# Batch 0 of a fused adapter and mixture-of-experts kernel: where its sums, its results and its small operands are kept, and when they are moved

## The reference, cut to what matters

```python
def reference(x, ids, lang, A0, B0, W, Wr, A, B):      # x: (8, 512, 2048) float32
    Bx = einsum('bni,bri->bnr', x, B0[ids])            # adapter of the batch element, rank 16
    x = x + einsum('bnr,bor->bno', Bx, A0[ids])        # first layer
    base = einsum('btd,od->bto', x, W)                 # W: (2048, 2048)
    logits = einsum('btd,ed->bte', x, Wr) + 5.0 * one_hot(lang, 8)[:, None, :]
    gates = softmax of the top 2 of 8 logits, scattered back to 8
    h = einsum('btd,erd->bter', x, A)                  # 8 experts of rank 16
    lora = einsum('bter,bte,eor->bto', h, gates, B)
    return x + base + 2.0 * lora                       # second layer
```

## Time and profile before

| | us |
|---|---|
| median of 3 runs | 1602.15 |
| lowest and highest | 1599.51, 1602.99 |
| the profiled execution's own time | 1606.35 |
| its span, first to last instruction | 1604.6 |
| PE busy (share of the span) | 1556.7 (97%) |
| DVE busy | 1221.7 (76%) |
| ACT busy | 713.9 (44%) |
| POOL busy | 126.2 (8%) |

### The profile page before, as it was taken

The page is one execution under the profiler, slowest core; times in us unless marked ns, Lnnn a source line. Parts: engine busy times, 40 slices in busy tenths (PEclk is TensorE's granted clock), DMA queues, the critical chain, the costliest instruction groups (busy, mean ns, idle before and its releaser), DMA issues.

```text
span 1604.6 us, 20300 instructions
## 1 busy us (share of the span) xinstructions
PE 1556.7 (97%) x7446; PEld 1308.1 (82%) x7446; DVE 1221.7 (76%) x1625; ACT 713.9 (44%) x908; POOL 126.2 (8%) x176
## 2 busy tenths in 40 slices
PE   8687999999999999999999999999999999999998
PEld 8565877888888888888888888888888888888887
DVE  5785675897678876987769976888769877797665
ACT  5432222254444544454444544455444544445443
POOL 1254454300000000000000000000000000000000
PEclk9898999999999999999999999999999999999999
DMA  9979998877677776677777776778866777576664
GB/s 235 254 212 233 220 267 211 231 223 220 199 238 218 227 221 204 223 217 225 207 221 229 218 217 199 229 218 237 217 211 221 212 229 203 190 235 201 206 221 159
DMA packets 332534, 351.37 MB, mean 219 GB/s; under 512 B 229834, under 2 KB 265978, under 8 KB 331642
## 3 DMA queue, kind: packets, MB, share of 16 engines
q1 hardware_dynamic: 323026, 318.61, 69.5%
q0 software_dynamic: 9136, 30.94, 6.1%
q10 hardware_dynamic: 272, 0.52, 0.1%
HBM read 280.75 MB, written 68.82 MB: 218 GB/s over the span
## 4 chain that ended last, share of the span: by engine, by line
PE 88%; DVE 5%; DMA 4%; ACT 1%; issue 1%; SPq 1%; POOL 0%; DVEq 0%; ACTq 0%; POOLq 0%
PE pb L808 26%; PE pb L809 26%; PE pb L810 26%; PE pb L372 4%; PE pb L374 3%; PE pb L526 2%; DMA xst<-in_x_dram 1%; DVE raw L674 1%; DMA t_scr<-ost 1%; DVE wl L804 1%; DMA b0n<-in_L_cond_B_dram 1%; ACT wh L800 1%; DVE pool_a L533 1%; SPq L659 0%; DMA an<-in_L_cond_A_dram 0%
## 5 line engine op out<-in xcount | busy, mean ns | idle before, releaser
L800 ACT CAST wh<-raw 128x1024 fp32r<-128x1024 f32 (+1 forms) x456 | 477.0, 1046 | 753.2 <-PE pb L810 738.0
L804 DVE TENSOR_TENSOR wl<-raw,wh 128x1024 fp32r<-128x1024 f32 (+1 forms) x456 | 559.6, 1227 | 286.6 <-ACT wh L800 285.2
L808 PE MATMUL pb<-wh,sh 128*128 128x512 f32 x1568 | 612.9, 391 | 0.5 <-DVE ost L846 0.5
L809 PE MATMUL pb<-wl,sh 128*128 128x512 f32 x1568 | 611.6, 390 | 0.0
L810 PE MATMUL pb<-wh,sl 128*128 128x512 f32 x1568 | 611.2, 390 | 0.0
L810 PEld LDWEIGHTS pb<-wh,sl 128*128 128x128 f32 x1568 | 294.3, 188 | 62.9
L808 PEld LDWEIGHTS pb<-wh,sh 128*128 128x128 f32 x1568 | 294.5, 188 | 56.3 <-DVE wl L804 0.9
L809 PEld LDWEIGHTS pb<-wl,sh 128*128 128x128 f32 x1568 | 294.6, 188 | 55.1
L372 PE MATMUL pb<-awb,xah 128*128 128x304 f32 x512 | 138.5, 304 | 0.0
L374 PE MATMUL pb<-awb,xal 128*128 128x256 f32 x512 | 134.4, 280 | 0.0
L808 PE MATMUL pb<-wh,xh 128*128 128x512 f32 x256 | 105.6, 413 | 16.3 <-DVE ost L846 14.4
(11 more groups left out here) (149 smaller groups left out, 1286.1 us busy)
## 6 DMA issues: line engine op xcount, KB each, us to landing
raw<-t_scr SPq DMA_DIRECT2D x392, 512.0 KB, 3.8
xst<-in_x_dram SPq DMA_DIRECT2D x448, 64.0 KB, 3.6
out_dram<-ost SPq DMA_DIRECT2D x72, 256.0 KB, 3.4
raw<-in_L_cond_W_dram SPq DMA_DIRECT2D x124, 128.0 KB, 4.7
raw<-bt_scr SPq DMA_DIRECT2D x28, 512.0 KB, 3.5
out_dram<-u SPq DMA_DIRECT2D x56, 256.0 KB, 2.8
t_scr<-tst POOLq DMA_DIRECT2D x17, 512.0 KB, 5.5
t_scr<-raw POOLq DMA_DIRECT2D x32, 256.0 KB, 4.6
```

The lines of the kernel that those rows point to most:

```text
L800: e.copy(pair_split(wh, g), pair_source(g)).then_inc(c_wh, 1)
L804: e.tensor_tensor(out=pair_split(wl, g), in0=pair_source(g), in1=pair_split(wh, g).bitcast(f32), op=ALU.subtract).then_inc(c_wl, 1)
L808: e.matmul(o, h, wh[:, g % RING, k, :], start=start, stop=False)
L809: e.matmul(o, h, wl[:, g % RING, k, :], start=False, stop=False)
```

## The change

All of it is in batch 0 and the part before it.

1. **Six banks.** The results of chunk c go to the banks `(0, 1, 2, 3, 6, 7)[(4 * c + t) % 6]`. PE needs nothing evacuated for t = 0 and 1 of the next chunk; for t = 2 and 3 it waits for the evacuation of t = 0 and 1 of the chunk before. The transposes and deltas of batch 1 that used bank 6 use bank 5 or wait for its evacuation.
2. **Evacuation in two parts.** t = 0 and 1 are evacuated at the end of the chunk's last slot as before, t = 2 and 3 two slots later, both into `ost[:, 0:2]`; the second part waits for the stores of the first.
3. **W's sums** alternate strictly between `tst` and `ost[:, 2:4]`. POOL makes its two sums from the second pair on, not from the fourth.
4. **Gated rows** of chunk 0 are read from `bt` itself, those of chunks 1 and 2 from `btx`, a place of their own (it lies over `bxt`), so that they no longer take a turn of a raw place of W. The load of pair 10 waits for the transpose of pair 7, where before it waited for the split of the gated rows.
5. **ACT** copies the first and third step of the experts' B before it rounds the next pair of W.
6. **DVE before slot 0**: the transpose of pair 0 is moved ahead, `aux_sum` ahead of the last `a0_lo`, and the four sums of pair 0 to just behind the transpose of pair 1. ACT's rounding of pair 0 and `aux_low` are moved ahead too.
7. **The difference** of the experts' B is made by POOL in slot 6, no longer by DVE in slot 3.
8. **SP** loads the x of batch 1 a slot earlier, and its first two blocks in halves over slots 4 to 7.

The diff, cut to its core:

```diff
@@ bx_transpose, bx_keep, hg_hi, delta
+        def bx_bank(n):
+            return 5 if n == 1 else 6
@@ hg_hi, n == 0
-                e.wait_ge(d_btd, 16)
+                e.wait_ge(d_gs, 32)
+                e.wait_ge(d_ag, 48)
@@
+        def raw_turn(g):
+            return w_number(g) - (g > 2)
+
         def raw_place(g):
-            return (g + 1) % 2 if 3 <= g < 8 else g % 2
+            return raw_turn(g) % 2
@@ first_load
-            elif g == 9:
-                e.wait_ge(c_wc, 2 * w_number(6) + 2)
-            elif g >= 3:
-                before = {3: 0, 4: 1, 8: 7}.get(g, g - 2)
-                if before % 9 == 8:
-                    e.wait_ge(c_wl, before + 1)
-                else:
-                    e.wait_ge(c_wc, 2 * w_number(before) + 2)
...
+            elif raw_turn(g) >= 2:
+                before = raw_turn(g) - 2
+                e.wait_ge(c_wc, 2 * (before + (before >= 2)) + 2)
@@
         def sum_place(g):
-            return (0, 0, 0, 1, 0, 1, 0, 1)[g] if g < 8 else (1, 0, 0, 1, 0, 1, 0, 1)[g % 9]
+            return w_number(g) % 2
@@ w_sum
-            return ost[:, 0:2, :].rearrange("p t (s n) -> p (t s) n", s=2) if sum_place(g) else tst[:, :, :]
+            return ost[:, 2:4, :].rearrange("p t (s n) -> p (t s) n", s=2) if sum_place(g) else tst[:, :, :]
@@ w_sums
-            if w < 3:
+            if w == 0:
@@ pair_source
-            return raw[:, g % 2, 0, :] if i % 9 == 8 else w_kept(g).rearrange("p a n -> p (a n)")
+            if i % 9 != 8:
+                return w_kept(g).rearrange("p a n -> p (a n)")
+            return (bt[:, 0:CW], btx[:, :], btx[:, :], raw[:, raw_place(g), 0, :])[i // 9]
@@
+        def first_bank(c, t):
+            return (0, 1, 2, 3, 6, 7)[(4 * c + t) % 6]
+
+        def wait_first(e, c, t):
+            e.wait_ge((c_evd, c_eva)[t % 2], 2 * c + 1 + t // 2)
@@ first_products
-                if c and k == 0 and h == 0:
-                    e.wait_ge((c_evd, c_eva)[t % 2], 2 * c - 1 + t // 2)
+                if k == 0 and h == 0 and c and t >= 2:
+                    wait_first(e, c - 1, t - 2)
+                elif k == 0 and h == 0 and c >= 2:
+                    wait_first(e, c - 2, t + 2)
@@ first_evacuate
-            if c:
-                e.wait_ge(d_ost[t // 2], 32 * c)
-            if t < 2:
-                e.wait_ge(d_ts[1], sums_in(1, min(9 * c + 10, SLOTS0)))
+            if c == 3 and t >= 2:
+                e.wait_ge(d_ts[1], sums_in(1, SLOTS0))
+            elif c or t >= 2:
+                e.wait_ge(d_ost[0], 32 * (2 * c + t // 2))
@@
+        EVACUATED = {8: (0, 0), 10: (0, 2), 17: (1, 0), 19: (1, 2), 26: (2, 0), 28: (2, 2)}
@@ act_main
-                pair_hi(e, i + 2)
                 if i in (1, 2):
                     bt_copy(e, 2 * i - 2)
+                pair_hi(e, i + 2)
```

More of the change, by code:

```diff
@@ L116, in adapted_moe_lora_kernel @@
         st48 = sb("st48", [P, TT, P], f32)
+        s4 = ExitStack()
+        btx = sb("btx", [P, CW], f32, s4)
+        s4.close()
         bxt = sb("bxt", [P, T], f32r)
@@ L407, in bx_transpose @@
             for t in range(TT):
-                last = e.transpose(pb[:, 6, t * P:(t + 1) * P], st48[:, t, :], ident[:, :])
+                last = e.transpose(pb[:, bx_bank(n), t * P:(t + 1) * P], st48[:, t, :], ident[:, :])
             last.then_inc(c_gp, 1)
@@ L414, in bx_keep @@
                 e.wait_ge(c_dl, 16 * n)
-            e.copy(bxt[:, :], pb[:, 6, :]).then_inc(c_ga, 1)
+            if n == 1:
+                e.wait_ge(c_wl, 27)
+            e.copy(bxt[:, :], pb[:, bx_bank(n), :]).then_inc(c_ga, 1)
         def aux_adapted(e, n):
@@ L611, in w_number @@
             return g // 9 * 8 + g % 9
+        def raw_turn(g):
+            return w_number(g) - (g > 2)
         def raw_place(g):
-            return (g + 1) % 2 if 3 <= g < 8 else g % 2
+            return raw_turn(g) % 2
         def raw_in(g):
-            return sum(32 if n % 9 == 8 else 64 for n in range(g + 1) if n != 2 and raw_place(n) == raw_place(g))
+            return sum(32 if n == SLOTS0 - 1 else 64 for n in range(g + 1)
+                       if n != 2 and (n % 9 != 8 or n == SLOTS0 - 1) and raw_place(n) == raw_place(g))
         def raw_before(s):
@@ L702, in wait_sum_place @@
                 e.wait_ge(d_ts[n], sums_in(n, g))
-            if g == 3:
+            if g == 1:
                 e.wait_ge(c_bnj, E)
-            if n and g % 9 == 3 and g > 9:
-                e.wait_ge(d_ost[0], 32 * (g // 9))
         def w_blocks(g):
@@ L713, in w_sums @@
             b11, b12, b21, b22 = w_blocks(g)
-            done = 4 * w if w < 3 else 2 * w + 6
+            done = 2 * w + 2 if w else 0
             e.wait_ge(c_wc, 2 * w + 2)
@@ L1156, in bt_half @@
             return bt[:, :].rearrange("p (c w n) -> p w c n", c=4, w=2)[:, w, :, :]
+        bt_diff = pool_a[:, 3, 0:4, :]
         def bt_difference(e):
             e.wait_ge(c_btc, 4)
-            e.wait_ge(d_gs, 32)
-            e.wait_ge(d_ag, 48)
-            e.tensor_tensor(out=late[:, :].rearrange("p (c n) -> p c n", c=4), in0=bt_half(0), in1=bt_half(1),
-                            op=ALU.subtract).then_inc(c_btc, 1)
+            e.wait_ge(c_l0, 16)
+            e.tensor_tensor(out=bt_diff, in0=bt_half(0), in1=bt_half(1), op=ALU.subtract).then_inc(c_btd, 1)
         def bt_store(e):
@@ L1170, in bt_difference_store @@
         def bt_difference_store(e):
-            e.wait_ge(c_btc, 5)
-            e.dma_start(bt_scr[:, 2, :], late[:, :]).then_inc(d_btd, 16)
+            e.wait_ge(c_btd, 1)
+            e.dma_start(bt_scr[:, 2, :].rearrange("p (c n) -> p c n", c=4), bt_diff).then_inc(d_btd, 16)
         def bias_columns(e):
@@ L1325, in pool_main @@
                 sums = i + 2 < SLOTS0 and (i + 2) % 9 != 8
-                if sums and i:
+                if sums:
                     w_sum_3(e, i + 2)
@@ L1329, in pool_main @@
                     w_store(e, i + 3)
-                if sums and i:
+                if sums:
                     w_sum_2(e, i + 2)
-                if sums:
                     w_sums_store(e, i + 2)
@@ L1622, in sp_main @@
                     pair_load(e, i + 6)
-                if i % 9 == 8:
+                if i in EVACUATED:
+                    for t in range(2):
+                        first_store(e, EVACUATED[i][0], EVACUATED[i][1] + t)
+                if i == 35:
                     for t in range(TT):
-                        first_store(e, i // 9, t)
+                        first_store(e, 3, t)
             for b in range(1, NB):
@@ L1643, in sp_main @@
             for c in range(2):
-                e.wait_ge(d_ost[c], 128 + 64 * (NB - 1))
+                e.wait_ge(d_ost[c], OST0[c] + 64 * (NB - 1))
                 e.wait_ge(d_u2[c], 32 * (NB - 1))
```

97 lines of the change are left out of this document (60 added, 37 removed).

## The result

The changed kernel takes 1584.08 us (median of 4 runs, 1581.45 to 1584.87) against 1602.57 us for the kernel before in the same session (4 runs, 1599.51 to 1605.93). The ratio is 0.9881, 95% interval 0.9858 to 0.9904: faster by 1.2%. The gain is 18.5 us between the medians, where 24.3 were forecast, and 1584.08 lies inside the range of 1565 to 1592.

A forecast was written before the change was run, and what follows sets the result against it. PE was taken as the bound, losing time only to waits and lower clock. Gains of 21.4 + 4.7 + 0.7 - 1.5 - 1.0 = 24.3 us from the 1602.15 median gave 1577.9, said as 1578; range 1565 to 1592.

The forecast's parts named there:

- The boundaries: Ends of chunks in batch 0: 4.7 of 6.7 us gained at the second, 0.7 at the third, nothing at the fourth.
- the slower rival: Slots 10, 19, 28: DVE waits for output stores, PE runs dry; could cost 28 us, giving 1606; chance 0.06.
- Slot 1: PE's 9.9 us wait for the copy of B goes entirely; DVE's split of pair 3 ends 7.5 us earlier, at 70.3.
- The start: Before slot 0: PE's first transpose and DVE's first adaptation, at 55.17 before, come 2.0 us earlier.
- my rivals: DMA becomes the bound 1588 (0.16); slot 1's wait renamed 1590 (0.10); more than forecast 1567 (0.08); slower 1606 (0.06).
- Chunk 0: Pair 3's split to gated rows' split takes 36.6 us; with start and slot 1, 25.4 us gained including 2.9 of clock.
- the term for POOL: Slot 6: POOL's long difference lengthens DVE's work, charged 1.0 us, bounds 0 and 3.0; four more sums counted as hidden.
- DMA: Batch 0: transfers limited near 267 GB/s take back 4 us in chunk 0 and 1.5 us in chunks 1 and 2.
- The sum: Whole kernel: 21.4 + 4.7 + 0.7 - 1.5 - 1.0 = 24.3 us gained.
- the start of slot 9 at 119.0: First slot of chunk 1: effective start at 119.0 in place of 141.5, before anything was taken off for DMA or POOL.
- the signs that I named: Batch 0, if right: PE idle 33 down to about 15 us, slot 9 near 118 to 123, 250 GB/s or more.

The follow-up runs named there:

- Experiment 8: Changed kernel with four PSUM banks for batch 0's results and all four tiles evacuated at the chunk's end, new places kept: 1613.09 us, ratio 1.0049 to the kernel before.
- Experiments 7: Changed kernel with ACT's old order, the copy of the experts' B behind the rounding of W: 1588.36 us, ratio 0.9898 to the kernel before.
- 9: Kernel before with only the alternating places of W's sums in chunk 0: 1601.11 us, ratio 0.9981 to the kernel before.
- 10: Kernel before with only ACT's order changed, the copy of the experts' B ahead of the rounding: 1601.63 us, ratio 0.9981 to the kernel before.
- experiment 1: The changed kernel again, with no edit, for a second profile: 1585.77 us, ratio 0.989 to the kernel before.
- Experiments 2: Changed kernel with the adapter rows' DMAs issued ahead of the load of the experts' B on SP: 1580.18 us, ratio 0.9857 to the kernel before.
- experiment 3: Changed kernel with DVE's transpose of pair 0 back in its old place before slot 0: 1581.99 us, ratio 0.9864 to the kernel before.
- experiment 4: Changed kernel with POOL's sums of chunk 0 over 4 columns, the rest left out: 1581.48 us, ratio 0.9857 to the kernel before.

## Why the forecast was nearly right

**The boundaries: right.** Four waits on evacuations, 14.9 us in all, became three with 2.3 (0.64, 1.11 and 0.5), the clock stayed up through chunks 1 and 2, and the second half of an evacuation never stood in PE's way. ACT in the changed kernel did wait for an output store, and it cost PE nothing:

```profile
ACT ost L879 <- DMA out_dram<-ost: 7.2, 2, 4.2
```

So the slower rival (an output store behind which DVE stops) did not come: DVE waited 0.2 us for one. Experiment 8 shows that it is real where the two slots between the halves are missing.

**Slot 1: the wait of PE right, the gain on DVE too large.** 9.9 us fell to 1.5, where nothing was to be left. Experiments 7, 9 and 10 say that the places of the sums and the order on ACT are each worth 1 to 3 us and that neither does it alone. But DVE became the bound, as forecast, and it was no earlier: the split of pair 3 ended at 77.6, 77.8 before. From the first adaptation on that is 19.2 us for 22.6, a gain of 3.4 where I had 7.5 - 2.0 = 5.5. The splits in between were 2.4 us longer than their twins, by POOL.

**The start: wrong.** I wrote that the first adaptation comes 2.0 us earlier, so at 53.2. It came at 58.44, 3.3 us later than 55.17, and in the profile of experiment 1 at 55.20, no earlier either. I counted the instructions of DVE that moved and not the DMAs that moved with them: the `a0g` rows stand in a queue behind a load, and pair 0's own traffic goes out earlier. From 50 to 58 us the DMA engines had a share of 1.23 and moved 151 GB/s. Experiments 2 and 3 take the two away one at a time, and PE's wait for the rows falls to 2.2 us and to nothing. This is a wait that none of my rivals named.

**Chunk 0: the term for POOL was mis-sized.** I took 36.6 us from the split of pair 3 to the split of the gated rows. It took 39.0 (77.6 to 116.6), and the slots before it too kept to DVE's cadence of 7.55 us, so that pair 3's split ended at 77.6 and not at 70.3. I charged 1.0 us, at most 3.0, for POOL's work beside DVE's, and set it in slot 6 alone. The row I had was one split of 1.55 in place of 1.22, and I treated it as an exception. The trace of before had seven such operations in chunk 0, and 3 us behind that row a dearer one, an x split of 2.37 in place of 1.29 beside the next sum on POOL:

```profile
95.32 2.37 DVE L553 TENSOR_TENSOR xl<-pool_a,xh 128x512 fp32r<-128x512 f32 x2
...
95.96 1.18 POOL L730 TENSOR_TENSOR ost<-raw 128x256 f32<-128x256 f32 x1
```

With the change four sums more, and in slot after slot, put two POOL operations on two of DVE's: 1.4 us in each slot, 7.7 in chunk 0 (experiment 4). The long difference took 2.40 us for 3.0 forecast, and the split beside it was 1.43 longer. Taken against their twins, DVE's lengthened operations add up to some 3.6 us in the chunk 0 of before and to 9.5 in that of the changed kernel. So the term is 5.9 us, where I charged 1.0.

By the Trainium skill ("SBUF — State Buffer", section "SBUF: two separate sides") whichever of the two starts first keeps the pair of ports for its whole instruction. The 2.40 us difference agrees: it started first and ended at 121.81, 1.56 us after the split began, and the split took 1.43 longer. The sums of 4 columns in experiment 4 agree too, the other way round: DVE's split started first, at 74.77, and kept its 1.23 us, and the sum beside it ended at 76.05, just behind it. The full short sums agree less well. The sum at 76.55 began 0.5 us behind the split of the pair, and the split was 0.3 longer all the same; in the x splits both engines lengthened, DVE by 1.1 us and POOL by 0.4.

**DMA: no bound of a rate.** The 4 us taken off chunk 0 and 1.5 off chunks 1 and 2 rested on 267 GB/s as a limit. Chunk 1 moved 271 GB/s over 57 us. Chunk 0 moved less, 235 GB/s, and DVE's work filled it. What DMA does cost is in when single loads come, which no sum of bytes shows, and it differs from one execution to the next: 5 us between the two profiles of the same kernel.

**The sum.** The forecast set the start of slot 9 at 119.0 (its begin at 117.8 and the 1.2 us of wait), with POOL and DMA at 124.0. By the same count it came at 128.47 + 0.64 = 129.1. So chunk 0 with the clock behind it gained 141.5 - 129.1 + 2.9 = 15.3 us for 20.4 forecast (21.4 - 1.0). From there to the last evacuation it was 318.36 - 141.5 - 2.9 = 174.0 before and is 295.37 - 129.1 = 166.3 now: 7.7 for 3.9 forecast (4.7 + 0.7 - 1.5). Together 23.0, of which 22.3 are seen, since the rest of the kernel took 0.6 us longer. Two errors of opposite sign, -5.1 and +3.8, met, and that is luck.

The -5.1 are the start (5.3) and POOL's term (5.9 - 1.0 = 4.9), less the 4.0 for DMA that were not lost; about 1 us is not accounted for. Of the +3.8, 1.5 are the DMA loss that did not come; 0.9 are at the second boundary, where 2.0 were to stay and a wait of 1.1 did; and about 1.7 are the clock behind the third: 54.32 x 0.06 = 3.3 us lost there before, 52.49 x 0.03 = 1.6 now. Against them stand the 0.5 us of wait left at the third.

The rest of the 6 us between 1578 and 1584 is in how executions scatter: I took before's profiled one 4.2 us down to its median, and the changed one lay at its own. Of the signs that I named, PE's idle time in batch 0 (33 us, now 14) and the 250 GB/s came; slot 9 near 118 to 123 us did not, it began at 128.5.

## What to carry to other kernels

When an edit moves an instruction, move on paper every DMA that it releases as well, and ask what stands ahead in that queue; the only new wait here came from there. When one engine bounds a stretch, look in its rows for an operation that is longer than its twins, and see what another engine does at that moment; here the trace of before showed such operations already. Timing POOL's sums to DVE's PSUM reads and transposes, together with the rows first, gave 7 to 11 us beside the 18.5 of the change. And an evacuation that shares a place with the one before needs the first one's stores to have landed: the new places lost time without the extra banks that put two slots in between.

## What was not expected of the hardware

A POOL sum of 128 x 256 takes 0.73 us by itself and 1.17 or 1.66 beside a DVE operation on two SBUF inputs, and DVE's take 1.55 for 1.22 and 2.37 for 1.29 (two). Cut to 4 columns in experiment 4, the POOL sum takes 0.78 us beside DVE's split and 0.21 at 97.27, where DVE is idle, and DVE's operations are as if alone. So there it is POOL that stands still, and its record is long by waiting, not by work:

```profile
75.27 0.78 POOL L756 TENSOR_TENSOR tst<-raw,tst 128x4 f32<-128x4 f32 x1
...
97.27 0.21 POOL L750 TENSOR_TENSOR tst<-raw 128x4 f32<-128x4 f32 x1
```

The same DMAs of adapter rows land in 4.7 to 5.4 us ahead of a load on their queue and in 8.0 to 11.4 behind it; but behind the same load it was 6.2 to 7.8 and 6.4 to 6.6 where pair 0 was transposed later (experiment 3, the kernel before). And the DMA engines moved 271 GB/s over 57 us, but 151 over 8 us at a higher share (1.23 against 1.08).
